# Twelve layers of linear attention on one core: two halves of the batches, interleaved by stage

## What is computed

```python
qkv = x @ Wqkv[i].T + bqkv[i]
q, k, v = jnp.split(qkv, 3, axis=-1)        # 16 heads of 8 channels
att = jnp.einsum('bhqd,bhkd->bhqk', q, k) * scale
y = jnp.einsum('bhqk,bhkd->bhqd', att, v)
x = y @ Wproj[i].T + bproj[i] + x
```

## Time and profile before

| | us |
|---|---|
| median of 3 runs | 340.52 (340.5 to 341.39) |
| the profiled execution | 344.02 |
| its span, first to last instruction | 342.1 |

### The profile page before, as it was taken

The page is one execution under the profiler, slowest core; times in us unless marked ns, Lnnn a source line. Parts: engine busy times, 40 slices in busy tenths (PEclk is TensorE's granted clock), DMA queues, the critical chain, the costliest instruction groups (busy, mean ns, idle before and its releaser), DMA issues.

```text
span 342.1 us, 8348 instructions
## 1 busy us (share of the span) xinstructions
PE 321.5 (94%) x3336; PEld 291.8 (85%) x3336; DVE 226.9 (66%) x638; ACT 183.2 (54%) x417; POOL 96.3 (28%) x89
## 2 busy tenths in 40 slices
PE   7899999999999999999999999999999959999994
PEld 6879889798897988979889797997979948888873
DVE  1057677775776757667587575776756717998974
ACT  3237858376583855738558385573850434433450
POOL 2005036050310504105050050500450302654533
PEclk9899999999999999999999999999999969999999
DMA  8651001010020200202001010110000000112112
GB/s 229 222 249 59 4 2 59 2 61 2 2 59 3 61 0 3 61 2 61 0 9 55 2 59 2 14 50 2 1 2 2 1 4 0 31 31 56 36 34 63
DMA packets 10660, 13.66 MB, mean 40 GB/s; under 512 B 512, under 2 KB 8832, under 8 KB 10496
## 3 DMA queue, kind: packets, MB, share of 16 engines
q1 hardware_dynamic: 8368, 11.94, 11.1%
q10 hardware_dynamic: 2256, 1.21, 1.3%
HBM read 11.04 MB, written 2.10 MB: 38 GB/s over the span
## 4 chain that ended last, share of the span: by engine, by line
PE 79%; DVE 8%; issue 4%; DMA 3%; ACT 2%; POOL 1%; ACTq 0%; POOLq 0%; DVEq 0%
PE ps L790 13%; PE ps L843 13%; PE ps L876 12%; PE ps L748 6%; PE ps L746 6%; PE ps L747 6%; PE ps L955 3%; PE ps L799 3%; DMA xt<-x_tok 3%; PE ps L829 3%; DVE s_rows L581 2%; PE ps L806 2%; DVE xt L681 2%; PE ps L944 2%; DVE mt L574 2%
## 5 line engine op out<-in xcount | busy, mean ns | idle before, releaser
L346 POOL TENSOR_TENSOR step_lo<-step,step_hi 128x512 fp32r<-128x512 f32 x44 | 54.8, 1279 | 182.3 <-ACT step_hi L430 182.3
L746 PE MATMUL ps<-state_hi,step_hi 128*128 128x258 f32 x176 | 50.7, 288 | 0.0
L843 PE MATMUL ps<-s_rows,w 32*128 32x256 f32 x768 | 44.8, 380 | 5.5 <-DVE s_rows L581 5.5
L748 PE MATMUL ps<-state_hi,step_lo 128*128 128x258 f32 x176 | 49.9, 283 | 0.0
L747 PE MATMUL ps<-state_lo,step_hi 128*128 128x258 f32 x176 | 49.6, 282 | 0.0
L843 PEld LDWEIGHTS ps<-s_rows,w 32*128 32x128 f32 x768 | 40.4, 185 | 7.4 <-ACT s_rows L424 7.4
L430 ACT CAST step_hi<-step 128x512 fp32r<-128x512 f32 x44 | 27.0, 619 | 33.7 <-DVE step L586 33.7
L790 PE MATMUL ps<-w,gram 128*128 128x128 f32 x352 | 44.0, 278 | 0.0
L790 PEld LDWEIGHTS ps<-w,gram 128*128 128x128 f32 x352 | 41.1, 192 | 1.0
L876 PE MATMUL ps<-step,gram 128*128 128x128 f32 x320 | 40.6, 281 | 0.0
L876 PEld LDWEIGHTS ps<-step,gram 128*128 128x128 f32 x320 | 37.3, 192 | 3.3 <-DVE step L586 3.3
(11 more groups left out here) (103 smaller groups left out, 509.9 us busy)
## 6 DMA issues: line engine op xcount, KB each, us to landing
w<-weights SPq DMA_DIRECT2D x12, 496.5 KB, 3.5
xchan<-x_chan SPq DMA_DIRECT2D x1, 2048.0 KB, 10.4
out<-xchan SPq DMA_DIRECT2D x7, 256.0 KB, 2.3
xt<-x_tok ACTq DMA_DIRECT2D x4, 256.0 KB, 8.5
xt<-x_tok SPq DMA_DIRECT2D x4, 256.0 KB, 5.3
fw_int<-ffn_weights SPq DMA_DIRECT2D x1, 576.0 KB, 4.7
out<-xchan SPq DMA_DIRECT2D x2, 128.0 KB, 1.9
cst<-consts ACTq DMA_DIRECT2D x1, 154.5 KB, 4.6
```

Source lines behind the costliest of these rows:

```text
L346: nc.gpsimd.tensor_tensor(group(step_lo, g), group(step, g), group(step_hi_f, g), ALU.subtract).then_inc(step_lo_ready, 1)
L746: nc.tensor.matmul(dst, l_hi, r_hi, start=True, stop=False)
L748: return nc.tensor.matmul(dst, l_lo, r_hi, start=False, stop=True)
L843: last = nc.tensor.matmul(n_banks(h)[:, k, :], w[r, s, WQ + P * i:WQ + P * (i + 1)], s_rows[r, h, i, :], start=i == 0, stop=i == QUADS - 1)
```

## The change

The diff reorders the stages of PE and DVE between the `gk` products and H, in every layer. On PE the first half now goes through means, tokens and `s` before the second half starts on them, with `gk_stage(3)` between its tokens and its `s`. `n_stage` takes a range of `i`, and its first half of the products for half 0 is issued ahead of `s_stage(1)`, the other behind it. `m_means(0)` waits for the first piece of `kdiag` only; the waits for `b_lo_ready` and the second piece move behind `s_stage(0)`. On DVE `take_s(0)` moves ahead of `take_blocks(1)`. ACT, POOL and SP are unchanged.

```diff
@@ -589,8 +589,8 @@
                 take_blocks(0)
+                take_s(0)
                 take_blocks(1)
-                take_s(0)
                 take_s(1)
@@ -832,17 +832,18 @@
-                def n_stage(h):
+                def n_stage(h, quads=range(QUADS)):
                     pe.wait_ge(s_low_half_ready, at(2, h + 1))
                     pe.wait_ge(s_high_half_ready, at(2, h + 1))
-                    for i in range(QUADS):
+                    for i in quads:
                         for k in range(QUADS):
                             r = slice(QUAD * k, QUAD * (k + 1))
                             last = nc.tensor.matmul(n_banks(h)[:, k, :], w[r, s, WQ + P * i:WQ + P * (i + 1)],
                                                     s_rows[r, h, i, :], start=i == 0, stop=i == QUADS - 1)
-                    last.then_inc(n_done, 1)
+                    if QUADS - 1 in quads:
+                        last.then_inc(n_done, 1)
@@ -850,20 +851,22 @@
                 gk_stage(1, pairs=(1,))
                 gk_stage(2)
-                gk_stage(3)
-                pe.wait_ge(b_lo_ready, at(PAIRS, PAIRS))
-                pe.wait_ge(kdiag_ready, at(2, 2))
+                pe.wait_ge(kdiag_ready, at(2, 1))
                 m_means(0)
-                m_means(1)
                 pe.wait_ge(gk_ready, at(GROUPS, 2))
                 m_tokens(0)
-                pe.wait_ge(gk_ready, at(GROUPS, GROUPS))
-                m_tokens(1)
+                gk_stage(3)
                 if last_layer:
                     pe.wait_ge(wp_chain, 3)
                 s_stage(0)
+                pe.wait_ge(b_lo_ready, at(PAIRS, PAIRS))
+                pe.wait_ge(kdiag_ready, at(2, 2))
+                m_means(1)
+                pe.wait_ge(gk_ready, at(GROUPS, GROUPS))
+                m_tokens(1)
+                n_stage(0, range(0, QUADS // 2))
                 s_stage(1)
-                n_stage(0)
+                n_stage(0, range(QUADS // 2, QUADS))
                 n_stage(1)
```

## The result

| | before | changed |
|---|---|---|
| median, us | 340.87 (11 runs) | 342.67 (11 runs) |
| profiled execution, us | 344.02 | 342.62 |
| its span, us | 342.1 | 340.8 |
| ratio to before | | 1.0041, 95% interval 1.0027 to 1.0055 |

The account below looks back on a forecast made before the run. PE's order of work and its holes bound the kernel; removing 0.90 us of waits but adding shape changes and a new wait loses 0.16 a layer, 340.52 + 2.0 = 342.5 us (own range 341.6 to 343.4; with B, C and D 339.8 to 344.8).

Parts of the forecast that it names:

- What bounds the kernel: Whole kernel: PE, busy 321.5 of 342.1 us, sets the end by its work's order and the holes in it.
- The waits that are removed: PE's waits for `mt` ahead of L829 (0.3) and `s_rows` ahead of L843 (0.6) go: 0.90 us a layer.
- The price of the changes of shape: PE tile-shape changes, seven instead of three: 0.19 us each to 128-column weights, about 0.12 to 32-column ones.
- Rival A: At shape changes the first load is pulled into the drain; H comes 0.28 us earlier a layer, 337.1 us; chance 0.14.
- B: Rival of no change: drains at shape changes cost 0.06 us, no loss elsewhere, 340.3 us; chance 0.22.
- C: Slower rival: L843 to L829 costs 0.19 us too, 0.35 a layer, 344.8 us; chance 0.15.
- The new wait ahead of `n_stage(1)`: PE must wait for the second half's `s_rows` copies before `n_stage(1)`: 0.22 us, plus a 0.10 reload.
- The queue on DVE: DVE work behind the second `take_s` ends 0.1 us before PE is ready for H: hidden, with hardly any cover.
- The sum: H comes 0.16 us later in each of 12 layers: +2.0 us, median 342.5, profiled execution 346.0.
- A sign that was set wrong: Prediction wrong if L829's second piece starts over 6.6 us after L815 (worse) or under 6.4 (better).

Follow-up runs that it names:

- x4: The changed kernel with n_stage(0) whole behind s_stage(1) instead of split around it: 346.56 us, ratio 1.0151 to before.
- x5: The changed kernel with gk_stage(3) moved back ahead of m_means(0): 347.77 us, ratio 1.0196 to before.
- x7: The changed kernel's order on PE with the old order on DVE, take_blocks(1) ahead of take_s(0): 357.45 us in a single run.
- y2: The changed kernel with one more unused 128x512 multiply on DVE between bqp and mbq: 347.68 us, ratio 1.0179 to before.
- x2: The kernel before plus three small unused matmuls of tile 32*128 in the H stage of each of 11 layers: 358.7 us.
- z3: The changed kernel with n_stage(0) cut 1 to 3 instead of 2 to 2 around s_stage(1): 340.69 us, ratio 0.9975 to before.
- x6: The changed kernel with bqp and mbq on DVE behind the first two add_identity instead of ahead: 342.69 us, ratio 1.0041 to before.
- w1: The kernel before without the branch ahead of the feed-forward part, keeping only the two-pass chunks: 335.28 us, ratio 0.9843 to before.

## Why the prediction was right

**What bounds the kernel.** Right: the runs moved by what H moved. x4, x5, x7 and y2 came out 5.4, 6.7, 16.2 and 6.4 us over before; 12 times the shift of H against 10.03 gives 5.2, 6.7, 17.2 and 6.0 (x7 is a single run).

**The waits that are removed.** Right: 5.5 us ahead of L843 became 0.5, none of it ahead of `n_stage(0)`, and x4 and x5 each brought a wait back.

**The price of the changes of shape.** This step decided the sign, and it stood on two rows, L815 to L790 and L843 to L876. The nine starts of the layer agree to 0.02 us, among them the pairs that before doesn't show (128*128 to 32*128 and 32*128 to 128*32). Rival A was wrong in its premise, B also: the drain is 0.093 in x2, not 0.06. C was wrong: L829 follows L843 at the plain step (from 171.560 to 171.775, 0.215).

**The new wait ahead of `n_stage(1)`.** Right in place and in size, 0.22 by the starts. z3 shows that 0.14 of this wait and its load could be had back by the place of the split, which is all of the loss. I had written it down as one term among several and had not asked whether it had to be there.

**The queue on DVE.** Hidden by 0.12, where I had 0.10; x6 and y2 show both sides of it.

**The sum.** 0.14 a layer was measured where 0.16 had been laid out. Half of the last 0.02 lies between the start of `n_stage(0)` and that of `s_stage(1)`, 0.968 where I had 0.98: I added the 0.02 by which four tiles are staggered though the shape stays there. The rest is spread over the other steps. With twelve layers that is 1.7 us, of which the last has 0.06 only, since before it had a hole of its own there: 1.6 us by the trace, 1.4 by the ratio, 1.8 between the medians. The forecast was +2.0, so it was 0.2 to 0.6 too high; that 342.5 and the measured 342.67 stand so close is in part luck, as the median of the kernel before rose from 340.52 in 3 runs to 340.87 in 11. For the profiled execution the prediction said 346.0 and it took 342.62, because the stretches outside the layers moved.

**A sign that was set wrong.** The prediction called itself wrong, and the kernel worse, if the second piece of L829 started more than 6.6 us after L815. Its own layout has it at 172.17 - 165.45 = 6.72, and 6.70 was measured. The layout was right and the bound didn't fit it.

## What to carry to other kernels

Filling a wait of TensorE with other work is worth the wait less the changes of tile shape it brings: here two waits of 0.9 us in all were filled; seven changes instead of three took about 0.7 of it back, and a new wait of 0.2 with a load of 0.1 behind it took the rest and a little more. Price a change from any place in the trace where the shape turns with nothing to wait for, lay the whole stage out in order, and look at what stands ahead of the last step, for that is where a small wait came back here. Read waits from starts: of 0.22 us only 0.04 was counted as idle. Try first to shorten the wait itself without leaving the shape: half a tile earlier from VectorE gave 0.13 us a layer for one more instruction.

## What the runs showed besides

The profile of the slower kernel was the shorter one because of two stretches that neither kernel touches. In front of the layers, the kernel before had 0.4 us more of waiting for `x_tok` and a lower granted clock. The columns are busy us of PE, its weight loads, DVE, ACT and POOL, then the granted clock, DMA share, GB/s; first before, then changed:

```profile
0.00:16.00 16.00, 12.56 (x80) 11.91 (x81) 1.40 (x3) 4.19 (x9) 2.19 (x8) 0.89 0.73 212
```

```profile
0.00:16.00 16.00, 12.95 (x96) 12.18 (x98) 1.76 (x6) 5.00 (x11) 2.19 (x8) 1.00 0.77 220
```

Behind the layers, ahead of the first chunk of the feed-forward part, where PE reads a flag and branches, PE stands idle and no semaphore releases it. The waits of PE, first before:

```profile
PE ps L944 <- issue: 4.1, 1, 4.1
```

then changed, and z3:

```profile
PE ps L947 <- issue: 3.8, 1, 3.8
```

```profile
PE ps L947 <- issue: 2.6, 1, 2.6
```

and six us from the idle time on, in windows with the same columns, for before, changed and z3:

```profile
274.00:280.00 6.00, 2.35 (x6) 1.88 (x7) 0.23 (x2) 1.23 (x5) 0.00 (x0) 0.75 0.03 5
```

```profile
274.00:280.00 6.00, 2.45 (x7) 1.96 (x8) 0.75 (x2) 2.04 (x7) 0.00 (x0) 0.86 0.02 5
```

```profile
272.00:278.00 6.00, 3.77 (x20) 3.19 (x21) 1.49 (x4) 3.26 (x9) 0.00 (x0) 1.00 0.01 3
```

With 4.1 and 3.8 us of idle time the granted clock is for a while at the lower of its two levels (1.2 of 2.4 GHz), from the end of the idle time on or just behind it; with 2.6 us it was not. Over 274 to 284 us it is 0.66 in the kernel before and 0.83 in the changed one. That is up to 1.7 us of PE's time by an estimate (0.17 of 10 us, a part of it while PE is idle), and with 0.3 us less idle time it makes up the 1.5 us behind the layers. The length of the idle time alone doesn't decide: before and x2 both wait 2.1 us for `x_tok`, and over the first 16 us the clock is 0.89 in one and 1.00 in the other. The layers, which have no idle time over 0.46 us in these three kernels, stand at 1.00 throughout.

```diff
-            flag = nc.values_load(low_flag[0:1, 0:1], engines=(pe.engine,), min_val=0, max_val=1)
-            with nc.If(flag != 0):
-                chunks(True)
-            with nc.Else():
-                chunks(False)
+            chunks(False)
```

> The kernel before, without the branch ahead of the feed-forward part: PE goes straight into the chunks with two passes, the variant with three passes for weights with a low part is left out. It asks where the spread between the profiles of one kernel sits. In the profiles PE stands idle 4.1 us (before), 3.8 (changed) and 2.6 (z3) ahead of the first matmul of the chunks with nothing released, and the granted clock of the 6 us around it is 0.75, 0.86 and 1.00; the layers agree to hundredths. Theory: the idle time belongs to the branch and draws the clock down behind it; without it the layers stay as they are, the idle time goes and the clock stays at 1.00 there: 4 to 6 us off before. If the idle time were the wait for ht_lo or other work: no change.

Measured: 335.28 us, ratio 0.9843 (0.9817 to 0.9868), 5.4 us off its before, and four runs within 0.8 us. The idle time is gone, the clock there is 1.00, and H stays at 10.03 in the layers:

```profile
272.00:278.00 6.00, 6.00 (x44) 5.45 (x43) 4.01 (x13) 3.35 (x9) 0.00 (x0) 1.00 0.00 0
```

Three times what the change of this study moved hangs on that branch. The idle time in the profile was 4.1 us; the rest of the 5.4 fits the lower clock behind it. The trace also shows what goes on meanwhile. In the kernel before, the only DMA transfer in the idle time (273.50 to 277.65) is one on the queue of instructions (kind, packets, MB, share):

```profile
q8 instruction: 1, 0.02, 1.9%
```

It has 16 KB, starts 1.02 us after PE went idle and takes 1.27 us, and PE goes on 1.85 us after its end. The same holds in all twelve traces that have the idle time: PE goes on 1.84 to 1.93 us after such a transfer ended. In eleven of them it starts 1.0 to 1.5 us into the idle time, which then lasts 3.8 to 4.3 us. In z3 it started 0.54 us ahead of it, and the idle time is 2.6 us. In w1 no such transfer lies there. So the idle time fits a wait for the code behind the branch; that is argued from the order in time, and no run moved the transfer by itself. Why it came early in z3 stays open. For a comparison of two profiles it means: read the stage that was changed, not the span.
